# A gated cross-attention block with routed experts on one core: 16-bit small sums in the prologue, moved table sums, an earlier shift transfer and a last tile in halves

## What is computed

```
x = x + tanh(g_xattn) * attention(layernorm(x), ctx, ctx)      # x (8, 512, 512), ctx (8, 120, 512), 16 heads of 32
    out    = softmax(Q K^T / sqrt(32)) V                       # Q, K, V with weights (512, 512) and biases
    expert = mean over 8 of (out @ We[e].T + be[e])            # folded to one matrix: mean of We, then Wo
    return expert @ Wo.T + bo
x = x + tanh(g_ffn) * ffn(layernorm(x))
    logits = x @ w_gate                                        # 8 experts; the best one per token
    locations = cumsum(one_hot(best)) - 1                      # only the first 100 tokens of each expert count
    out of those tokens: gate * (x @ w_expert + b_expert)      # all other rows stay as they are
```

## Time and profile before

| | us |
|---|---|
| median of 3 runs | 416.38 |
| lowest and highest of them | 416.18, 416.67 |
| the profiled execution's own time | 416.97 |
| its span (first to last instruction) | 415.5 |
| PE busy | 405.2 (98% of the span) |
| DVE busy | 332.8 (80%) |
| ACT busy | 227.6 (55%) |
| POOL busy | 166.2 (40%) |

### The profile page before, as it was taken

One profiled execution on the slowest core, in us unless ns is written; L12 is line 12 of the kernel. 1 busy time (PEld: TensorE's weight loads), 2 busy tenths in 40 slices (PEclk: granted clock), 3 DMA queues, 4 the chain that ended last, 5 costly groups with the idle time before them and its releaser, 6 DMA issues.

```text
span 415.5 us, 8770 instructions
## 1 busy us (share of the span) xinstructions
PE 405.2 (98%) x3122; PEld 191.7 (46%) x3122; DVE 332.8 (80%) x678; ACT 227.6 (55%) x318; POOL 166.2 (40%) x153
## 2 busy tenths in 40 slices
PE   8999999999999999999999999999999999999996
PEld 4566564444444344444434443443444444354442
DVE  7439346886797889988988998899896688579994
ACT  5435322569466754947585585748556473785100
POOL 2029999015080247309033530803261072550460
PEclk9999999999999999999999999999999999999999
DMA  8999971365058407723960683286059026231683
GB/s 266 340 390 396 390 291 35 89 120 161 2 113 184 174 0 163 213 96 88 174 208 2 141 227 101 65 175 232 2 128 235 6 51 175 71 115 34 118 175 137
DMA packets 64853, 63.19 MB, mean 152 GB/s; under 512 B 41225, under 2 KB 44437, under 8 KB 64811
## 3 DMA queue, kind: packets, MB, share of 16 engines
q1 hardware_dynamic: 59667, 56.18, 48.9%
q0 software_dynamic: 1632, 3.49, 3.1%
q10 hardware_dynamic: 3512, 2.97, 2.1%
HBM read 29.59 MB, written 12.98 MB: 102 GB/s over the span
## 4 chain that ended last, share of the span: by engine, by line
PE 78%; DVE 9%; POOL 4%; issue 4%; DMA 2%; ACT 1%; SPq 0%; DVEq 0%; POOLq 0%; ACTq 0%
PE ps L828 60%; PE ps L449 10%; PE ps L398 3%; PE ps L580 3%; DVE bn_raw L1450 2%; POOL known L1893 1%; POOL std L1902 1%; POOL rstd L1893 1%; DMA raw<-in_L_xattn_Wk_dram 1%; DMA q_stack<-shift 1%; DVE base_cnt L1619 1%; DVE rows L1789 1%; ACT xb L1215 1%; DVE bn_raw L1540 1%; DVE xb L1534 1%
## 5 line engine op out<-in xcount | busy, mean ns | idle before, releaser
L1215 ACT ACTIVATE probs<-ps 120x1024 f32<-120x1024 f32 x64 | 62.0, 1023 | 22.6 <-PE ps L828 22.6
L1568 DVE TENSOR_REDUCE neg_max<-ps 128x16 bf16<-128x1920 f32 x32 | 68.6, 2144 | 4.1 <-PE ps L828 4.1
L1952 POOL TENSOR_TENSOR attn_lo<-attn,attn_hi 128x512 f16<-128x512 f32 x28 | 31.8, 1157 | 95.9 <-ACT attn_hi L1215 95.9
L828 PE MATMUL ps<-xnT_hi,wqT_hi 128*128 128x512 f16 x128 | 48.6, 380 | 0.0
L828 PE MATMUL ps<-mixT_hi,attn_hi 128*128 128x512 f16 x128 | 48.6, 380 | 0.0
L828 PE MATMUL ps<-mixT_lo,attn_hi 128*128 128x512 f16 x128 | 48.5, 379 | 0.0
L828 PE MATMUL ps<-xnT_lo,wqT_hi 128*128 128x512 f16 x128 | 48.5, 379 | 0.0
L1960 POOL TENSOR_TENSOR xb<-xb,mix_bias 128x512 f32<-128x512 f32 x32 | 39.6, 1270 | 18.7 <-DVE cb_col L1511 18.7
L1215 ACT ACTIVATE q_hi<-ps,bias_cols 128x512 f16<-128x512 f32 x32 | 22.0, 687 | 35.3 <-PE ps L828 35.3
L828 PE MATMUL ps<-q_stack,k_stack 97*120 97x512 f16 x128 | 34.7, 390 | 0.9 <-DMA q_stack<-shift 0.8
L828 PE MATMUL ps<-probs,den_sel 120*32 120x256 f32 x512 | 34.1, 384 | 0.0
(11 more groups left out here) (270 smaller groups left out, 791.7 us busy)
## 6 DMA issues: line engine op xcount, KB each, us to landing
xb<-in_x_dram SPq DMA_DIRECT2D x8, 1024.0 KB, 6.0
q_stack<-q_hi SPq DMA_DIRECT2D x48, 128.0 KB
out_dram<-xb SPq DMA_DIRECT2D x6, 1024.0 KB, 6.0
raw<-in_L_xattn_We_dram SPq DMA_DIRECT2D x5, 1024.0 KB, 11.1
q_stack<-q_lo SPq DMA_DIRECT2D x32, 128.0 KB
xb<-in_L_xattn_We_dram SPq DMA_DIRECT2D x3, 1024.0 KB, 10.4
k_stack<-k_scratch SPq DMA_DIRECT2D x8, 360.0 KB, 4.3
out_dram<-xb SPq DMA_DIRECT2D x8, 256.0 KB, 2.1
```

What stands on the lines that cost most here:

```text
L828: return e.matmul(out_, a, b, start=start, stop=stop, **kw)
L1215: return e.activation(out_, in_, func, **kw)
L1568: e.tensor_reduce(neg_max[:, :, :, g], quad[:, :, 0:NT * SK].rearrange("p j (t s) -> p t j s", t=NT), AX.X, ALU.max, negate=True).then_inc ...
L1952: e.tensor_tensor(attn_lo[:, g, :], attn[:, g, :], attn_hi[:, g, :], ALU.subtract).then_inc(s_alo, 1)
```

## The change

- **Prologue, small sums.** `w_gate` is loaded straight into the tile `wg`, 128 partitions with four runs of 32 bytes each, and no longer turned by PE (the unit `wg`, 8 transposes, is gone); it is issued after Wv instead of before. The sum over `be`, the `fold` of `wogT`, and `mix_bias` read 16-bit pairs where they read 32-bit tiles. So `wogT` and `bias_part` are evacuated as pairs by ACT and DVE, where ACT alone wrote `partT`, and ACT and DVE each make one part of `be`. `v_unit(0)` moves ahead of the units `woT`; the fold moves behind two `x_unit`s. Waits that are implied by others are left out of `v_unit(7)` and the `mix` units.
- **Steady batches.** `places` moves from between `q_begin` and `q_end` to behind `q_end`; on DVE `choose` moves ahead of `logit_scale`, and `read_places` behind a third `x_lo`.
- **Last batches.** SP issues the last shift row too, ahead of two stores. `places` of batch 6 writes another bank (`num_b`), and no longer waits for the table (`s_tab`). `table_values` moves ahead of a `weight_sums`, the last `logits` into the middle of a `mix_high`.
- **End.** The last tile's expert product, its sum and its store are made in two halves of 256 columns.

```diff
+LAST_PARTS = [(t, slice(0, D)) for t in range(NT - 1)] + [(NT - 1, slice(h * D // 2, (h + 1) * D // 2)) for h in range(2)]
...
             unit(("v", b_), pe,
                  needs_of(*[("wvT", k) for k in range(NK)], *ctx_tiles(b_, b_ + 1)) + [(s_const, 16 * N_CONST)]
-                 + ([(s_last, 2)] if b_ == B - 1 else []),
+                 if b_ < B - 1 else [(s_last, 2)],
...
-                    ins = e.matmul(b[:, k:k + 1], be_sb[:, k * P:(k + 1) * P], ones_col[0:NE, :],
-                                   start=True, stop=True)
+                    for part in be_parts:
+                        ins = e.matmul(b[:, k:k + 1], part[:, k * P:(k + 1) * P], ones_16[0:NE, :],
+                                       start=(part is be_parts[0]), stop=(part is be_parts[1]))
...
-                for i in range(NE):
-                    ins = e.transpose(b[:, i * NK:(i + 1) * NK], wg_rows[:, :, i], ident[0:NK, 0:NK])
...
             unit("wogT", pe, needs_of("wg_mean") + [(s_wt["woT"][i], 16) for i in range(NK)],
-                 act=lambda e, b: e.activation(partT[:, :], b[:, :], ACT.Copy))
+                 **pair_evac(*wog_parts, lambda b: b[:, :], GATE_SCALE))
+
+        def fold_parts(e, b):
+            for k in range(NK):
+                for part in wog_parts:
+                    ins = e.matmul(b[:, k * NE:(k + 1) * NE], part[:, k * P:(k + 1) * P], gate_sum16[:, NE:2 * NE],
+                                   start=(part is wog_parts[0]), stop=(part is wog_parts[1]))
+            return ins
...
-                unit(("mix", k), pe, needs_of(*[("woT", o) for o in range(NK)]) + [(s_sumh, 1), (s_suml, k + 1)]
+                unit(("mix", k), pe, [(s_suml, k + 1)]
...
-        k_units(1, [gate_rows_unit, be_unit, gate_and_mean])
+        k_units(1, [be_unit, gate_and_mean])
         weight_units("wqT", pair=(wqT_hi, wqT_lo), scale=QK_SCALE)
+        v_unit(0)
         weight_units("woT", pair=(woT_hi, woT_lo), scale=OUT_SCALE)
-        v_unit(0)
         gate_out_rows_unit()
...
-            load(wg_rows.rearrange("k p e -> k (p e)"), w_gate.rearrange("(k p) e -> k (p e)", p=P), s_const)
-            load(be_sb[:, :], be, s_const)
+            load(be_sb[:, :], be, s_be)
             load_tiles("wvT", Wv)
+            load(wg[:, :, :], w_gate.rearrange("(k p) e -> p k e", p=P), s_wg)
...
-                    if r < B - 2:
-                        e.wait_ge(s_sh, r + 2)
-                        load(q_stack[3 * DK:STACK, :, :, :].rearrange("o j g s -> o (j g) s"),
-                             shift[:, :], s_rsh)
+                    e.wait_ge(s_sh, r + 2)
+                    load(q_stack[3 * DK:STACK, :, :, :].rearrange("o j g s -> o (j g) s"),
+                         shift[:, :], s_rsh)
                     if r == B - 2:
                         store_tiles(r, (0, 1))
...
-                if b == B - 2:
-                    e.wait_ge(s_x1, 4 * b + 3)
-                    e.wait_ge(s_tab, b)
-                elif b < B - 2:
+                if b < B - 2:
                     e.wait_ge(s_pxe, b + 3)
...
-                (places, -1, 0), (q_end, 1, 0), (values, 0, 2), (values, 0, 3), (max_scores, 1, 0),
+                (q_end, 1, 0), (places, -1, 0), (values, 0, 2), (values, 0, 3), (max_scores, 1, 0),
...
-                (values, 0, 1), (scores, 0, 3), (weight_sums, 0, 2), (table_values, -1, 0), (value_sums, 0, 2),
+                (values, 0, 1), (scores, 0, 3), (table_values, -1, 0), (weight_sums, 0, 2), (value_sums, 0, 2),
...
-                (mix_high, 0, 2), (mix_low, 0, 2), (logits, 0, 0), (mix_high, 0, 3), (mix_low, 0, 3),
+                (mix_high, 0, 2), (mix_low, 0, 2), (mix_begin, 0, 3), (logits, 0, 0), (mix_middle, 0, 3), (mix_low, 0, 3),
...
-                (logit_gap, -1, 0), (logit_scale, -1, 0), (choose, -1, 0), (x_lo, 2, 0), (x_lo, 2, 1), (gate_mix_low, 0, 0), (read_places, -1, 0),
-                (x_lo, 2, 2), (q_low, 1, 0), (x_lo, 2, 3),
+                (logit_gap, -1, 0), (choose, -1, 0), (logit_scale, -1, 0), (x_lo, 2, 0), (x_lo, 2, 1), (gate_mix_low, 0, 0),
+                (x_lo, 2, 2), (read_places, -1, 0), (q_low, 1, 0), (x_lo, 2, 3),
...
-                e.scalar_tensor_tensor(out=row, in0=quad[:, t, :], scalar=last_coef[:, t:t + 1], in1=row,
+                row = xb[:, b % NX, t, cols]
+                e.scalar_tensor_tensor(out=row, in0=last_bank(i)[:, cols], scalar=last_coef[:, t:t + 1], in1=row,
                                        op0=ALU.mult, op1=ALU.add).then_inc(s_lo, 1)
```

More of the change, by code:

```diff
@@ L353, in build @@
         s_ls = sem("s_ls")
-        SET, SETV, N_CONST = 15, 21, 3
-        wg_rows = part_x[0:NK, :, :].rearrange("k a s -> k (a s)").rearrange("k (p e) -> k p e", e=NE)
+        SET, SETV, N_CONST = 16, 21, 1
+        be_parts = [a[0:NE, 1, :] for a in (sum_hi, sum_lo)]
+        bias_parts = [a[:, 0, :] for a in (sum_hi, sum_lo)]
+        wog_parts = [a[:, 2, :] for a in (sum_hi, sum_lo)]
         units, made, late = [], {}, []
@@ L503, in mean @@
                 return e.matmul(b[:, 0:NE], ones_col[:, 0:1].to_broadcast([P, P]), wg_over[:, :], start=True, stop=True)
-            unit("wg_mean", mean, needs_of("wg") + [(s_set, 5)],
+            unit("wg_mean", mean, [(s_wg, 17), (s_set, 5)],
                  dve=lambda e, b: e.scalar_tensor_tensor(
@@ L541, in gate_out_unit @@
         def gate_out_unit():
-            unit("wog", fold, needs_of("wogT") + [(s_setv, 11)],
+            unit("wog", fold_parts, needs_of("wogT") + [(s_setv, SETV - 2)],
                  dve=lambda e, b: e.tensor_scalar(wog[:, :, NE:2 * NE],
                                                   b[:, 0:NK * NE].rearrange("p (o e) -> p o e", o=NK),
-                                                  ATTN_SCALE * MIX_SCALE, None, ALU.mult))
+                                                  ATTN_SCALE * MIX_SCALE * PART_SCALE / GATE_SCALE, None, ALU.mult))
         def gate_bias_unit():
@@ L565, in bias_part_unit, with pe @@
             unit("bias_part", pe, needs_of("be_col", "wog", *[("woT", k) for k in range(NK)]),
-                 act=lambda e, b: e.activation(partT[:, :], b[:, :], ACT.Copy))
+                 **pair_evac(*bias_parts, lambda b: b[:, :], 1.0 / OUT_SCALE))
         def mix_bias_unit():
-            unit("mix_bias", lambda e, b: e.matmul(b[:, :], ones_col[:, 0:1].to_broadcast([P, P]), partT[:, :],
-                                                   start=True, stop=True),
+            def pe(e, b):
+                for part in bias_parts:
+                    ins = e.matmul(b[:, :], ones_16[:, 0:1].to_broadcast([P, P]), part,
+                                   start=(part is bias_parts[0]), stop=(part is bias_parts[1]))
+                return ins
+            unit("mix_bias", pe,
                  needs_of("bias_part") + [(s_bo, 16)],
                  dve=lambda e, b: e.scalar_tensor_tensor(out=mix_bias[:, :], in0=b[:, :],
-                                                         scalar=1.0 / (DK * BIAS_SCALE * OUT_SCALE), in1=bo_bc[:, :],
+                                                         scalar=1.0 / (DK * BIAS_SCALE), in1=bo_bc[:, :],
                                                          op0=ALU.mult, op1=ALU.add))
@@ L1148, in row_turn, with expert3 @@
                 ins.then_inc(s_tt, 1)
[L1150 to L1153 removed]
+            def expert3(bank, hi, lo, steps_of=slice(None), cols=slice(0, D)):
+                steps = [(hi(k), b(k)) for k in range(NK) for b in (lambda k: wqT_hi[:, k, cols], lambda k: wqT_lo[:, k, cols])]
+                steps += [(lo(k), wqT_hi[:, k, cols]) for k in range(NK)]
                 for i, (a, b) in list(enumerate(steps))[steps_of]:
@@ L1250, in first_rows, with be_part_high @@
                         bias=x0_shift[:, t:t + 1]).then_inc(s_xn, 1)
+            def be_part_high():
+                e.wait_ge(s_be, 16)
+                act(be_parts[0], be_sb[:, :], scale=BIAS_SCALE / NE).then_inc(s_be, 1)
             for i in range(N_FIRST):
+                if units[i]["done"] == made[("wvT", 2)]:
+                    be_part_high()
                 if units[i]["done"] == made["wogT"]:
@@ L1479, in _ @@
             for i in range(N_FIRST):
+                if units[i]["done"] == made[("wvT", 2)]:
+                    be_part_low()
+                    gate_over()
                 prepare(0, i)
```

73 lines of the change are left out of this document (37 added, 36 removed).

## The result

The changed kernel takes 414.47 us in the median of ten runs, against 416.34 for the kernel before (ten runs): a ratio of 0.9943, 95% interval 0.9927 to 0.9959. The forecast was 411.0 with a range of 409 to 413. The sign was right, the size was a third of it, and the range was missed.

A forecast was written before the change was run, and what follows sets the result against it. PE, busy 405.2 of 415.5 us, was taken as the bound; prologue 1.7, steady batches 2.75, last batches 0.45 and end 0.5 sum to 5.4 off the profiled 416.97, giving a median of 411.0, range 409.0 to 413.0.

The forecast's parts named there:

- E: Prologue: the end of ACT's issues of K's stores, forecast between 47.05 and 48.3; `cb` was to start at E + 7.8.
- the fold's lead: Prologue: of the 2.5 us PE is ahead at the fold, 0.7 survives as gain, bounds 0 to 1.2.
- The slower rival: Prologue: K's stores hold ACT, each us on E beyond 48.3 costs PE one; 417.7 us, chance 0.04.
- The absorption: Prologue: waiting for ACT and DVE at the fold takes back most of PE's 2.5 us lead; 0 to 1.2 survive.
- the small sums: Prologue: dropping `wg` saves 1.0, the 16-bit sum of `be` 0.8, the fold some 0.7; 2.5 if no wait arose.
- mix_bias: Prologue: its two 512-column products in 16 bits instead of 32 take 0.43 us off.
- "issue" gaps: Prologue: gaps of 0.4 and 0.3 ahead of `v_unit(7)` and the first `mix` close; 0.6 taken, 0 to 0.7.
- Steady batches, last batches, end: Behind the prologue: five `base_cnt` waits save 2.75 us, the last batches 0.45, the halved last tile 0.5.
- place_hot: Last batches: of 1.2 us in closed gaps nearly all returns as PE's wait for this DVE result; 0.15 kept.
- the last shift row: Last batches: issued by SP ahead of two stores, it lands 2.1 us after issue and its 0.8 wait goes.
- The half sum: End: DVE's last sum on 256 columns takes 0.38 us instead of 0.75; 0.25 saved if a fixed part stays.
- `w_gate`'s pieces: Prologue: 512 pieces of 32 bytes delay POOL's sums by 1.7 to 68.65, costing nothing; rival 411.7 to 412.5, chance 0.08.

The follow-up runs named there:

- v0_back: The changed kernel with `v_unit(0)` put behind the `woT` units again: 411.0 us (410.43 to 411.54).
- rest_only: The changed kernel with the old prologue and all other parts of the change: 412.93 us (412.74 to 413.40).
- last_batches: The kernel before with the changes to the last batches alone: 417.08 us against 421.82, ratio 0.9870.
- stores_by_sp: The changed kernel with the second half of K's stores issued by SP instead of ACT: 409.86 us, ratio 0.9836.
- filled: The changed kernel with 11 products that nothing reads put into PE's waits ahead of the first `x_unit` and the fold: 413.13 us (412.21 to 422.06).
- again2: The changed kernel, unchanged, timed again on the third group's chip: 414.59 us (413.40 to 416.79).
- before_again: The kernel before, unchanged, profiled on the fourth group's chip: 421.9 us.
- again: The changed kernel, unchanged, timed once more in the first group: 413.52 us (411.75 to 415.88).

## Why the prediction was wrong

**The step that failed** is the fold's, in two places. One is "`cb`, which needs that, starts at E + 7.8". In the three profiles of the changed kernel `cb` starts 9.8 to 10.0 behind E, the end of ACT's issues (49.99 to 59.97, 48.15 to 57.96, 49.24 to 59.00). The other is "The last issues would end at 48.3 at the old pace of 2.39 / 4 = 0.6; at the median of 0.49 nearer 47.05". E was 49.99 in the profiled run and 48.15 and 49.24 in the two others: the issues began at 41.6 to 41.7 instead of 41.1, and the twelve took between 6.6 and 8.3 us. Over all of K's stores the median issue stayed at 0.45 to 0.48; the longest single one took 0.73 in the quickest of the three and 1.33 and 1.34 in the others. The two paces of one trace were taken as bounds, and they aren't. So the term of 0.7 for the fold's lead, bounds 0 and 1.2, was -3.9, -1.9 and -2.9 in the three profiles.

From the forecast's `cb` at 55.4 to the measured 59.97 are 4.6 us. E was 2.3 later than the middle of my range (49.99 against 47.68). The clock took 1.7: waits on PE of 0.8, 2.2 and 0.4 stood within 6 us, and it fell. No term had that in it. The last 0.5 is a chain that I had chosen wrongly: from the fold on I followed DVE's list. That list was right, as DVE has `wog` ready at 57.66, which is E + 7.7:

```profile
57.48 0.18 DVE L547 TENSOR_SCALAR wog<-ps 128x32 f32<-128x32 f32 x1
```

But PE's own list ends later. The fold starts at E + 4.8, behind it come a gap of 0.4 and the twelve products of `v_unit(4)`, and at full clock, in `v0_back`, `cb` is at 54.79 - 46.49 = 8.3 behind E. The sum is 4.5. The gap of 0.4 isn't explained: the profile names DVE's `v_all` for it in one kernel and ACT's `xnT_hi` in another, but by the list of units `v_unit(4)` waits for neither, only for a bank of `woT` that was free long before.

The slower rival had the right place, and its price, "Each us on E beyond 48.3 costs PE one", holds between the three profiles: E differs by 1.84 at most and `cb` by 2.01. What it had wrong is where the loss starts. At E = 48.15 `cb` was already 1.9 behind the kernel before.

**The absorption** as such was foreseen, but as a lead that shrinks to nothing at worst; it turned into a delay. With the stores off ACT 2.3 of it arrive, so the small sums were sized well. In the changed kernel the eight products on `be` start at 26.93 to 27.12, a spacing of 0.03, and `mix_bias` goes from 64.91 to 65.35, 0.44 against a forecast of 0.43. Both "issue" gaps, 0.7 in sum, are gone from the table; 0.6 was taken.

**Steady batches, last batches, end:** 2.75 + 0.45 + 0.5 = 3.7 forecast, 3.7 measured (`rest_only`, where before took 416.6). The sum is shown, its parts only in so far as the profile shows the waits. `place_hot` and the last `base_cnt` took back what the other waits gave, as forecast. One step of it failed unseen: the last shift row was to land 2.1 after its issue "like the other seven". It landed 3.0 after in the changed kernel's profile, where PE had no wait for it, and 4.0 to 4.2 in `v0_back`, `last_batches` and `stores_by_sp`, where PE waited 0.7, 0.8 and 1.1. ACT's own took 4.2 before. That cost little, since the shift row's wait and the one for `place_hot` stand in for each other: in `stores_by_sp` they are 1.1 and 0.2, in the changed kernel 0 and 1.0. The half sum was taken at 0.38 and took 0.48, so DVE gave 0.27 instead of 0.38.

**The wait at `row_turn`** was left out, as in the trace at hand it was 0.2. On two other chips the profiles show 2.0 to 3.6 in that stretch, and on a third the time of before, 420.8, points to the same. There the change is worth more: `v0_back`, `filled` and `again2`, on two of those chips, have no wait at that place. That didn't enter the result, for which before took 416.3. Why the same program stands there in most runs on some chips isn't settled. In `before_again` PE is idle for 2.6 there, DVE for 2.3 and ACT for 3.05, which the profile puts down to "issue" and "remote"; POOL meanwhile issues gathers, one every 1.4. No run here tells the gathers, the loading of instructions and other causes apart.

**`w_gate`'s pieces:** POOL's last sum ends at 68.72 against the 68.65 worked out, and nothing waited for it. That the two agree is luck. In ten profiles of kernels with the pieces that sum ends at 67.13 to 68.83, in eight without them at 66.91 to 68.09, so a delay of 1.7 isn't there; the means are 0.5 apart.

**The chances:** I gave the clock none. For the slower rival I gave 0.04 and asked for an average issue of 1.0. An average of 0.69 was enough to lose the whole gain of the prologue, and so was 0.55, in `again`.

## What to carry to other kernels

A gain on the bounding engine ahead of an in-order engine's block of issues arrives only if that block ends earlier too; moving one unit ahead of what releases the block cost 2.5 to 3.6 us here, read across chips, and giving the block to another queue brought 3.7 on one chip and 5.0 on another. Where several waits on PE come close together, count them twice: once as themselves, and once as what the clock may lose behind them (1.8 in the median here). From a point where one engine's result is ready, follow every engine's list to the next meeting, and not only the one that looks busiest. If the times of a kernel spread while its rival's don't, look at the granted clock of each run and at what its engines issue before the terms of the sum. A wait of 0.2 in one trace was 2 or more on other chips here, so it can be worth taking away.

## What the runs showed of the hardware

The granted clock fell after three waits of 0.78, 2.16 and 0.42 between small pieces of work, and in `again` after two of 1.75 and 0.42. It stayed low while PE was fully busy with the next seven or eight products. One such fall cost 1.5 to 1.7 us in the three profiles of the changed kernel. Products whose results nobody reads, put in the waits, kept it up in eleven of twelve runs. An issue of the same K transfer took ACT 0.5 to 0.7 us on average over twelve, differing by run and by stretch within one kernel. The last shift row landed 3.0 to 4.2 us after its issue, where the median of the same transfer in the other batches is 2.1, whichever engine issued it. A DVE sum on 256 columns took 0.48 where 512 took 0.75, so 0.2 of it doesn't scale.
